# A graph layer's last edge group moved into the scan of the message table

## What is computed

```
h       = relu(layernorm(x))
z       = concat(h[src], h[dst], edge_attrs)
gated   = sigmoid(z @ W_f + b_f) * softplus(z @ W_s + b_s)
message = segment_sum(gated, src, num_segments=100000)
normed  = (message - mean(message)) * rsqrt(var(message) + 1e-5) * gamma + beta
out     = x + h + normed          # mean and var per column, over all nodes
```

## Time and profile before

| | |
|---|---|
| median of 3 runs | 1072.77 us (1071.25 to 1073.52) |
| the profiled execution, its own time | 1070.97 us |
| its span in the trace | 1069.2 us |
| mean granted clock of TensorE | 0.608 |
| busy, TensorE | 638.0 us, 60% |
| busy, VectorE | 734.3 us, 69% |
| busy, ScalarE | 543.7 us, 51% |
| busy, GpSimd | 711.3 us, 67% |
| DMA | 175.63 MB, 164 GB/s on average |

### The profile page before, as it was taken

One profiled execution on the slowest core, in us unless ns is written; L12 is line 12 of the kernel. 1 busy time (PEld: TensorE's weight loads), 2 busy tenths in 40 slices (PEclk: granted clock), 3 DMA queues, 4 the chain that ended last, 5 costly groups with the idle time before them and its releaser, 6 DMA issues. The chain is left out here.

```text
span 1069.2 us, 10789 instructions
## 1 busy us (share of the span) xinstructions
PE 638.0 (60%) x2340; PEld 451.1 (42%) x2340; DVE 734.3 (69%) x1557; ACT 543.7 (51%) x1187; POOL 711.3 (67%) x612
## 2 busy tenths in 40 slices
PE   0436776657755677666576656466666696854332
PEld 0224544445534455444364444344545585620000
DVE  3846886668675767666686656466757638999788
ACT  0425665646655556545466455446454645634232
POOL 7775777877778787777787777887778650040600
PEclk9995665555556555555555565556555659955555
DMA  8997543534544334333344343433333269999999
GB/s 279 416 397 267 128 125 76 124 78 121 124 103 98 86 54 86 87 54 86 54 85 86 55 86 57 82 54 87 53 84 42 20 217 422 379 283 428 414 408 387
DMA packets 87410, 175.63 MB, mean 164 GB/s; under 512 B 41922, under 2 KB 48646, under 8 KB 78928
## 3 DMA queue, kind: packets, MB, share of 16 engines
q1 hardware_dynamic: 34727, 111.07, 28.8%
q0 software_dynamic: 42176, 19.83, 16.4%
q10 hardware_dynamic: 10472, 44.38, 10.2%
HBM read 106.98 MB, written 68.24 MB: 164 GB/s over the span
## 5 line engine op out<-in xcount | busy, mean ns | idle before, releaser
L536 POOL DMA_INDIRECT m_buf<-in_x_dram,m_buf x392 | 376.2, 960 | 120.7 <-issue 112.8
L549 POOL DMA_INDIRECT msgs_dram<-m_buf,target x188 | 295.3, 1571 | 69.4 <-issue 56.4
L1015 PE MATMUL ps_all<-m_buf 128*128 128x64 f32 x940 | 198.2, 402 | 160.1 <-DVE m_buf L756 83.5
L1015 PEld LDWEIGHTS ps_all<-m_buf 128*128 128x128 f32 x940 | 190.6, 311 | 172.0 <-issue 156.1
L648 DVE TENSOR_REDUCE m_buf<-m_last 128x24 f32<-128x1536 f32 x49 | 85.7, 1749 | 52.7 <-ACT m_last L864 52.7
L997 PEld LDWEIGHTS ps_all<-sums,m_buf 128*128 128x128 f32 x392 | 94.7, 331 | 50.6 <-issue 50.6
L912 ACT ACTIVATE m_buf<-m_buf,one_col 128x512 f32<-128x512 f32 x196 | 107.6, 550 | 1.6
L983 PE MATMUL ps_all<-ident,m_buf 128*128 128x128 f32 x196 | 54.3, 432 | 89.4 <-DVE m_buf L716 89.3
L864 ACT ACTIVATE m_last<-m_buf 128x1536 f32<-128x1536 f32 x49 | 72.2, 1473 | 60.0 <-DVE m_buf L619 60.0
L995 PE MATMUL ps_all<-sums,m_buf 128*128 128x512 f32 x98 | 101.7, 1141 | 0.0
L619 DVE SCALAR_TENSOR_TENSOR m_buf<-ps_all,m_buf 128x1024 f32<-128x1024 f32 x98 | 93.9, 958 | 3.9
(11 more groups left out here) (152 smaller groups left out, 994.7 us busy)
## 6 DMA issues: line engine op xcount, KB each, us to landing
m_buf<-msgs_dram SPq DMA_DIRECT2D x38, 1024.0 KB, 17.0
m_buf<-in_x_dram SPq DMA_DIRECT2D x48, 512.0 KB
out_dram<-m_buf ACTq DMA_DIRECT2D x20, 1024.0 KB, 11.3
msgs_dram<-y_kept SPq DMA_DIRECT2D x11, 1536.0 KB
m_buf<-src_rows_dram SPq DMA_DIRECT2D x46, 256.0 KB, 4.0
y_spill_dram<-y_kept ACTq DMA_DIRECT2D x19, 512.0 KB, 4.0
y_kept<-y_spill_dram SPq DMA_DIRECT2D x8, 1024.0 KB, 17.4
msgs_dram<-y_kept ACTq DMA_DIRECT2D x5, 1536.0 KB
```

The lines of the kernel that those rows point to most:

```text
L536: pool.indirect_dma_start(xg[:, n % G_SLOTS, 2 * j + c, :], None, x, bass.IndirectOffsetOnAxis(ap=ids[:, c, n * TILES + j:n * TILES + j + ...
L549: pool.indirect_dma_start(msgs, bass.IndirectOffsetOnAxis(ap=target[:, n % UNROLL, j:j + 1], axis=0), comb[:, n % COMB_SLOTS, j, :], None, ...
L1015: pe.matmul(ps_c[:, j, :], same_of(b, j, j + 1)[:, 0, :], msg_of(g)[:, b, :], start=(b == 0 and not joined), stop=(b == j), skip_group_che ...
```

## The change

Group 48 leaves stage one's pipeline and is worked on beside the scan.

- **Gathers.** PRE = 48 groups are gathered in steps. Group 48's eight gathers go behind the others, two after each of two scatter waits and four behind the last scatter group, into a buffer of their own. LATE is 3: group 46 is kept back too, so the late tiles are twelve.
- **Its work.** VectorE, ScalarE and TensorE each do a piece of group 48 behind or inside a scan block: VectorE centres behind block 4, sums squares behind 5, scales behind 6, multiplies the softplus behind 10, and takes targets and the sum of messages behind 17. ScalarE does its parts between the second and third square of blocks 5, 6, 8, 10, 11 and 17. TensorE turns behind block 7, has the products behind 8, and combines behind 16.
- **Joining.** Group 48 must be joined with the eight tiles of groups 46 and 47. VectorE makes eight masks of 512 columns, alternating two buffers, behind blocks 8 to 15 (`mask_last`), TensorE has a join of four products for each (`join_last`).
- **Squares.** Stage one's PSUM is still in use, so the squares use two banks (6, 2) up to block 17 and three (6, 4, 5) from block 18. Blocks 8 to 18 have 18 rows squared instead of 20 and seven crossings instead of six. The other five banks are blanked behind block 17.
- **SP.** The ring has five buffers; 5, 6 and 7 are used first by blocks 21, 22 and 23. Block 21 waits also for group 48's message, 22 for its masks, 23 for its combined sum and for the correction. Block 3 waits for group 47's combined sum and group 48's gathers.
- **GpSimd** makes the correction's products (768 columns) and the row list; VectorE keeps the reduction, behind block 20. S_SLOTS is 2, DRAIN 2, and y's early copies move from block 12 to 18.

The diff, cut to what is spoken of:

```diff
-DRAIN = 3
+DRAIN = 2
-S_SLOTS = 3
+S_SLOTS = 2
-LATE = 2
+LATE = 3
+PRE = GROUPS - 1
...
+SCAN_BUFS = 5
 SQ_ROWS = 20
-SQ_BANKS = (5, 6, 4)
+SQ_BESIDE = 18
+BESIDE = range(8, 19)
+SQ_FIRST = (6, 2)
+SQ_THEN = (6, 4, 5)
+SQ_CHANGE = 18
-Y_BLOCK = 12
+Y_BLOCK = 18
 Y_AHEAD = 4
-LIST_AT = 6
-CORRECT_AT = 8
+FINISH_AT = 17
+CORRECT_AT = 20
...
+        def gather_last(tiles):
+            for j in tiles:
+                for c in range(2):
+                    pool.indirect_dma_start(
+                        xg_last[:, 2 * j + c, :], None, x,
+                        bass.IndirectOffsetOnAxis(ap=ids[:, c, LAST * TILES + j:LAST * TILES + j + 1], axis=0),
+                    ).then_inc(last_gathered, 16)
+
...
+        pool.wait_ge(ids_rest, 64)
         for n in range(behind, EARLY):
+            gather_last([n - behind])
             accumulate(n)
+        gather_last(range(EARLY - behind, TILES))
...
-        def later_in_last():
+        def mask_last(t):
+
+            k, b = divmod(t, TILES)
+            slot = g_last.slot(S_SLOTS)
+            if t == 0:
+                dve.wait_ge(src_loaded[slot], 16 * g_last.uses(S_SLOTS) + 16)
+                dve.wait_ge(z_turned, GROUPS)
+            elif t == 1:
+                dve.wait_ge(v_done, GROUPS)
+            else:
+                dve.wait_ge(mask_used, t - 1)
+            dve.scalar_tensor_tensor(
+                out=cross_last[t % 2], in0=src_all[:, slot, :, :],
+                scalar=own[:, g_last.back(LATE - 1 - k).slot(UNROLL), b:b + 1],
+                in1=ones[:, :].unsqueeze(1).to_broadcast([P, TILES, P]), op0=ALU.is_equal, op1=ALU.mult,
+                accum_out=in_last[:, k, b:b + 1]).then_inc(mask_made, 1)
...
+        def join_last(t):
+
+            pe.wait_ge(mask_made, t + 1)
+            if t == 0:
+                pe.wait_ge(comb_copied, PRE)
+            for j in range(TILES):
+                ins = pe.matmul(ps_c[:, j, :], cross_last[t % 2][:, j, :], late_msg[:, t, :],
+                                start=(t == 0), stop=False, skip_group_check=True)
+            ins.then_inc(mask_used, 1)
...
+        sp.wait_ge(z_turned, PRE)
         for b, (r0, _) in enumerate(BLOCKS):
             if b == FREE_FIRST:
-                sp.wait_ge(sum_kept, 1)
+                sp.wait_ge(comb_copied, PRE)
+                sp.wait_ge(last_gathered, 16 * GATHERED)
+                sp.dma_start(m_rest[:, :], msgs[P * N_ROWS:NODES, :]).then_inc(rest_loaded, 16)
+            if b < NB - 1 and before_in_buf(b):
+                sp.wait_ge(rows_squared, chunks_of(before_in_buf(b)[-1]))
+                sp.wait_ge(block_crossed, before_in_buf(b)[-1] + 1)
+            if b < NB - 1 and scan_buf(b) == SCAN_BUFS:
+                sp.wait_ge(msg_done, GROUPS)
+            if b < NB - 1 and scan_buf(b) == SCAN_BUFS + 1:
+                sp.wait_ge(mask_made, (LATE - 1) * TILES)
+            if b < NB - 1 and scan_buf(b) == SCAN_BUFS + 2:
                 sp.wait_ge(comb_copied, GROUPS)
-                sp.dma_start(m_rest[:, :], msgs[P * N_ROWS:NODES, :]).then_inc(rest_loaded, 16)
-            if M_BUFS <= b < NB - 1:
-                sp.wait_ge(rows_squared, chunks_of(b - M_BUFS))
-                sp.wait_ge(block_crossed, b - M_BUFS + 1)
+                sp.wait_ge(corr_done, 1)
             for j, (r, n, _) in enumerate(pieces(b)):
                 sp.dma_start(m_scan(b, r, n), m_rows[:, r0 + r:r0 + r + n, :]
-                             ).then_inc(last_loaded[j] if b == NB - 1 else m_loaded[b % M_BUFS], 16)
+                             ).then_inc(last_loaded[j] if b == NB - 1 else m_loaded[scan_buf(b)], 16)
...
-                act.wait_ge(rows_added, k - len(ps_sq) + 1)
+            if added_before(k):
+                act.wait_ge(rows_added, added_before(k))
+            if r == BANK_ROWS:
+                if b == 5:
+                    last.square()
+                elif b == 6:
+                    last.rstd()
+                elif b == 8:
+                    last.copy_turned()
+                elif b == 10:
+                    last.softplus_log()
+                elif b == 11:
+                    last.gates()
+                elif b == FINISH_AT:
+                    last.copy_comb()
...
+        pe.wait_ge(y_done, STEPS)
         pe.wait_ge(blank_set, 1)
-        for bank in range(PSUM_BANKS - 1):
+        for bank in SQ_FIRST:
             ins = clear(bank)
         ins.then_inc(banks_blank, 1)
...
+            if b == 7:
+                last.turn()
+            elif b == 8:
+                last.products()
+            elif b == 9:
+                last.join(0)
+            elif 11 <= b < 16:
+                last.join(b - 10)
+            elif b == 16:
+                last.join(6)
+                last.join(7)
+                last.combine()
+            elif b == FINISH_AT:
+                pe.wait_ge(sum_kept, 1)
+                pe.wait_ge(comb_copied, GROUPS)
+                for bank in sorted(set(range(PSUM_BANKS - 1)) - set(SQ_FIRST)):
+                    ins = clear(bank)
+                ins.then_inc(banks_blank, 1)
...
+        def correct():
+
+            pool.wait_ge(late_read, 16 * LATE_TILES)
+            pool.tensor_tensor(was_read, was_read, was_read, ALU.add).then_inc(corr_steps, 1)
+            pool.wait_ge(corr_steps, 1)
+            pool.wait_ge(comb_copied, GROUPS)
+            pool.tensor_tensor(was_read, was_read, late_comb[:, :, :], ALU.add).then_inc(corr_steps, 1)
+            pool.wait_ge(corr_steps, 2)
+            pool.tensor_tensor(was_read, was_read, late_comb[:, :, :], ALU.mult).then_inc(corr_steps, 1)
...
+            pool.wait_ge(corr_steps, 3)
+            pool.wait_ge(nodes_marked, 1)
+            pool.tensor_tensor(was_read, was_read, marked[:, :].unsqueeze(2).to_broadcast([P, LATE_TILES, F]),
+                               ALU.mult).then_inc(corr_steps, 1)
...
+            dve.wait_ge(corr_steps, 4)
             dve.tensor_reduce(corr_row[:, :], was_read.rearrange("p t f -> p f t"), AX.X, ALU.add
                               ).then_inc(corr_done, 1)
...
+            if k + 1 < chunks_of(b):
+                continue
+            if b == 4:
+                last.centre()
+            elif b == 5:
+                last.sum_squares()
+            elif b == 6:
+                last.normalise()
+            elif b == 8:
+                last.mask(0)
+            elif b == 10:
+                last.mask(1)
+                last.softplus()
+            elif b == 11:
+                last.message()
+                last.mask(2)
+            elif 12 <= b < 15:
+                last.mask(b - 9)
+            elif b == 15:
+                last.mask(6)
+                last.mask(7)
+            elif b == FINISH_AT:
+                last.finish()
+                take_means()
+            elif b == CORRECT_AT:
                 correct()
```

439 lines of the change are left out of this document (270 added, 169 removed).

## The result

The changed kernel takes **1076.60 us** (median of 7 runs, 1076.43 to 1077.30) against 1072.97 of before (7 runs, 1071.25 to 1074.36): ratio 1.0036, 95% interval 1.0027 to 1.0046. The change makes the kernel slower by 3.6 us. That is small (0.4%), but its fastest run, 1076.43, lies above the slowest of before, 1074.36. Its profiled execution took 1077.09 us, with a span of 1075.4, which is 6.2 more than the span of before.

The account below looks back on a forecast made before the run. VectorE was taken to bound the scan (57 of 60 us busy or in handovers), DMA nearly even. Terms -10.0 - 3.2 + 6.7 + 2.7 + 3.3 + 0.3 + 3.4 + 0.3 gave +3.5 us, 1076.3; range 1066.5 to 1083.

Parts of the forecast that it names:

- Start of computing: Before the scan: first addition of squares at 864.1 instead of 874.05, joins over at 858, a gain of 10.0 us.
- Rival 2: Joins and handover: TensorE is fast there, joins end at 855 and handover costs 2.4, so -0.4 us, 1072.4; chance 0.25.
- VectorE's moved work: In the scan: group 48's work comes in, row list and correction products go out; cost 6.7 us, bounds 4.7 and 8.2.
- GpSimd's products beside VectorE's lists: Late in the scan: GpSimd's three correction products, some 5 us, cost nothing at anything up to 12 us.
- ScalarE's work between squares: In the scan: ScalarE's parts of group 48 make VectorE wait; cost 2.7 us, bounds 0.5 and 4.2.
- The handover: Blocks 16 to 18: TensorE's join, combining and blanking of five banks hold the squares; cost 3.3 us, bounds 2.4 and 7.6.
- End of the scan: Block 23's load must wait for the correction's reduction behind block 20; cost 0.3 us.
- the 3.2 of waits that went: In the scan: VectorE falls behind the loads, so its earlier waits there go; gain 3.2 us.
- Behind the scan: Output stage: twelve late adds for eight delay SP's reloads, cost 3.4 us; four more patches cost 0.3.
- 1: Scan: the moved work falls into VectorE's handovers, so the change is faster, -4.6 us, 1068.2; chance 0.28.
- 3: Scan: TensorE at 1.2 GHz becomes the bound, +16.5 us, 1089.3; chance 0.05 together with upper ends.
- The waits announced for blocks 10 and 18: A sign that the forecast is right: VectorE waits for ScalarE at these two scan blocks; no size given.

Follow-up runs that it names:

- e7: The change with two late groups for three, the sum of messages made first and GpSimd's products waiting for VectorE's last targets; 1068.04 us, 0.9959 of the kernel before.
- e1: The change with GpSimd's three products waiting until VectorE has made the last targets; 1073.43 us, 1.0024 of the kernel before.
- e2: The change with VectorE making the sum of messages first, not last, in the finishing piece behind block 17; 1073.73 us, 1.0017 of the kernel before.
- e3: The change with GpSimd's products waiting for VectorE's last targets and the sum of messages made first; 1070.71 us, 0.9992 of the kernel before.
- e5: The change with the correction's three products put back on VectorE, the row list staying on GpSimd; 1076.21 us, 1.0035 of the kernel before.
- e4: The change without group 46's four late adds (eight for twelve), its output lacking those messages; 1073.72 us, 1.0025 of the kernel before.
- e8: The change without group 46's four late adds and four output patches, its output lacking those messages; 1072.60 us, 1.0014 of the kernel before.
- e11: The change with two late groups for three, sum of messages still last and GpSimd's products at once; 1070.07 us, 0.9990 of the kernel before.

## Why the prediction was right, and where not

**The time.** 1076.3 was said and 1076.6 measured. Part of that is luck: the profiled spans differ by 6.2 us where the sum said 3.5, and the medians by 3.6, because the profiled execution of before lay 2.0 us below its median and that of the change 0.5 above. Within the 6.2 errors of both signs met: the hold-up that the prediction lacked added 3.0 and, by the clock, 1.1; the start was 0.7 worse than said and the rest of the handover 0.5; the moved work was 1.3 and ScalarE's work 1.2 cheaper.

**Start of computing.** Said -10.0, found -9.3; masks done at 847.1 (846.6 was said), joins over at 859.6, near the 859.0 of the half clock, of which I took 858. Right, and the choice of the half clock over the one row at 1.00 was the right reading. Two errors met here: the joins' end was 1.6 us later than the 858 of the sum, and ScalarE's part behind it took 5.1 us for 6.1, since the loads of gamma and beta were issued while it compared. Rival 2 falls with it. That SP's early start would mostly not be collected was right too; e7, with the loads 9.7 us later, is the faster kernel.

**VectorE's moved work.** Said 6.7, found 5.4: 8.4 us more busy, less the 3.0 of the next point. The 6.7 were a balance of 8.2 less 1.5 of handovers given back. VectorE's idle time apart from its waits for ScalarE is 6.3 us where it was 6.4, so none was given back there. What was saved is in the additions: one by one they sum to 40.1 us instead of 41.6, mostly by the shorter third pieces, which the prediction counted as nothing.

**The step that failed: GpSimd's products beside VectorE's lists.** The prediction put "anything up to 12 us for its three costs nothing". It asked whether GpSimd would be done in time and did not ask what VectorE does meanwhile. The products took 1.80, 1.80 and 1.47 us, 5.1 together (5 was the estimate from the Trainium skill's page), well in time; and two small operations of VectorE were held 3.0 us by the first two of them. Behind that TensorE stood still for 4.96 us, and its blanking at clock 0.50 took 1.06 us more than in e1, e2, e3 and e5, where it stood still for at most 1.97. The change, e4 and e8, the three traces with 4.96, all show 2.31 for the blanking. What the prediction put at nothing cost 4.1 us. The Trainium skill has the rule, on the page *SBUF — State Buffer*, section "SBUF: two separate sides": a VectorE operation with two SBUF inputs, or in a mode that uses two ports, and a GpSimd operation that reads SBUF exclude each other for the whole instruction, and who starts first keeps the port. The traces of e1, e3 and e5 agree: held where they overlap, 0.16 where not, and additions with one operand in PSUM never held. The runs show when operations are held; that a port is the reason is the page's.

**ScalarE's work between squares.** Said 2.7, found 1.5: waits of 0.34 and 1.14, before the first and the third piece of block 10. The 1.14 is the softplus chain, for which 1.4 was said; VectorE waits for none of the four smaller pieces, for which the prediction had 1.3.

**The handover.** Said 3.3, found 4.9 (0.27, 2.03 and 2.55), inside its bounds of 2.4 and 7.6. Of the 2.55, 1.06 belongs to the step that failed: with no hold-up, e5 waits 1.49 there. The 2.55 stands behind the lists, because the sum that allows the blanking was the last thing made in them; e2 gets it back by order alone.

**End of the scan.** Said 0.3, found 0.3. With the 3.2 of waits that went, -3.2 + 5.4 + 3.0 + 1.5 + 4.9 + 0.3 = 11.9; the scan grew by 11.8.

**Behind the scan.** Said 3.4 for late adds and 0.3 for patches, found 3.75 in sum. The sum is right, and the shares are not: e4 gives the adds 1.2 to 2.1.

**Rivals.** 1 said that VectorE's handovers would take the moved work in; its idle time grew instead. 3, TensorE at 1.2 GHz throughout, did not come: the clock is 0.93 on average over the scan, and 0.50 in stretches only, the blanking one of them. The waits announced for blocks 10 and 18 are there, and the adds' end 26.5 us behind the scan's (27 to 28 was said).

## What to carry to other kernels

Before work is moved onto an idle engine, look for what the busy engine does in the same microseconds: here GpSimd's products cost nothing beside VectorE operations with a PSUM operand, and held those whose operands were all in SBUF for what was left of the product. Count also what stands behind the one that is held: here TensorE's clock fell while it waited. In a piece that ends a stage, make first what the next engine waits for. And an early start is worth only as much as the stage behind it can use: one late group fewer started the loads 9.7 us later, the computing 1.2, and with its four masks, joins and late adds gone it made the kernel faster.

## What the runs showed of the hardware

A VectorE operation on 128x4 that takes 0.16 us elsewhere took 1.56 and 1.75 when a GpSimd product of 768 columns had begun before it. An operation with one SBUF input (L1664, 128x64) was held as well, 1.66 us in e1, while a reduction from PSUM (L911 in e2, 0.42 us at 911.23, beside the product of 910.96) and the additions with a PSUM operand kept their times. The GpSimd product that met a VectorE operation with two SBUF operands, begun just before it, grew from 1.80 to 2.30 (e3). TensorE was at granted clock 0.50 all through the 12.3 us of joins, products and sums right ahead of the squares, although it was busy in all of them, and at 1.00 in the scan before. At the handover it was at 0.50 behind 4.96 us without work (the change, e4, e8: five blanks in 2.31 us), and at 1.00 behind 1.97 and 1.96 us (e1, e5: 1.25) and 3.15 us (e11: 1.25).
